# Softmax attention on one core: values projected for two groups of heads at once, laps over groups written out

## The reference

```python
H, Hk, D = (NUM_HEADS, NUM_KV_HEADS, HEAD_DIM)      # 16, 4, 128
G = H // Hk
xq = (inputs_q @ wq + bq).reshape(B, S, H, D)
xk = (inputs_q @ wk + bk).reshape(B, S, Hk, D)
xv = (inputs_q @ wv + bv).reshape(B, S, Hk, D)
...
qg = (xq * scale).reshape(B, S, Hk, G, D)
attn = jnp.einsum('bqhgd,bkhd->bhgqk', qg, xk)
attn = jax.nn.softmax(attn.astype(jnp.float32), axis=-1).astype(xq.dtype)
out = jnp.einsum('bhgqk,bkhd->bqhgd', attn.astype(xv.dtype), xv)
out = out.astype(og_dtype).reshape(B, S, H * D)
return out @ wo + bo
```

## Time and profile before

| | |
|---|---|
| time, median of 3 runs | 1144.16 us (1141.73 to 1145.95) |
| profiled execution, first to last instruction | 1142.5 us, so 1.7 us below the median |
| TensorE busy | 1058.0 us, 93% of the span |
| VectorE, ScalarE, GpSimd busy | 758.7, 599.1 and 561.4 us |
| mean granted clock of TensorE | 0.973 of full speed |

### The profile page before, as it was taken

One profiled execution on the slowest core, in us unless ns is written; L12 is line 12 of the kernel. 1 busy time (PEld: TensorE's weight loads), 2 busy tenths in 40 slices (PEclk: granted clock), 3 DMA queues, 4 the chain that ended last, 5 costly groups with the idle time before them and its releaser, 6 DMA issues. The chain is left out here.

```text
span 1142.5 us, 18205 instructions
## 1 busy us (share of the span) xinstructions
PE 1058.0 (93%) x6276; PEld 891.7 (78%) x6276; DVE 758.7 (66%) x1312; ACT 599.1 (52%) x1027; POOL 561.4 (49%) x408
## 2 busy tenths in 40 slices
PE   5899999999999999999998899997977988999992
PEld 4788888888888888888886776654765787999992
DVE  4877764787556775667775644466788655777777
ACT  3566653666536665446662423433532255777772
POOL 1664622756236563355540347762314776544453
PEclk9999999999999999999999999998998989999996
DMA  7700240002400762000000146641200457666666
GB/s 196 52 28 1 58 36 3 19 11 38 56 2 24 207 218 69 1 1 1 1 2 24 58 137 212 215 136 56 106 2 6 161 191 240 207 221 219 225 212 199
DMA packets 45642, 109.94 MB, mean 96 GB/s; under 512 B 8519, under 2 KB 26069, under 8 KB 43504
## 3 DMA queue, kind: packets, MB, share of 16 engines
q1 hardware_dynamic: 38640, 95.46, 30.2%
q0 software_dynamic: 6912, 13.30, 3.1%
HBM read 94.27 MB, written 41.29 MB: 119 GB/s over the span
## 5 line engine op out<-in xcount | busy, mean ns | idle before, releaser
L422 POOL TENSOR_TENSOR at_prob<-at_prob,at_inv_sum 128x1024 f32<-128x1024 f32 x128 | 243.6, 1905 | 287.9 <-DVE at_inv_sum L647 287.9
L612 ACT ACTIVATE at_pt_h<-ps 128x512 fp32r<-128x512 f32 x256 | 139.1, 596 | 148.7 <-PE ps L537 148.6
L697 DVE TENSOR_TENSOR at_pt_l<-ps,at_pt_h 128x512 fp32r<-128x512 f32 x256 | 164.6, 685 | 60.8 <-ACT at_pt_h L612 60.7
L686 DVE TENSOR_REDUCE at_neg_max<-ps 128x1 f32<-128x1024 f32 x128 | 156.1, 1220 | 42.1 <-PE ps L41 41.7
L579 ACT ACTIVATE at_prob<-ps,at_neg_max 128x1024 f32<-128x1024 f32 x128 | 143.7, 1123 | 18.1 <-DVE at_neg_max L686 18.1
L537 PE MATMUL ps<-ident,at_prob 128*128 128x128 f32 x1024 | 133.8, 274 | 3.8 <-POOL at_prob L422 3.8
L2072 POOL DMA_INDIRECT lines<-f_y,f_x_raw x96 | 95.8, 998 | 82.7 <-ACT f_y L1990 54.7
L537 PEld LDWEIGHTS ps<-ident,at_prob 128*128 128x128 f32 x1024 | 120.0, 141 | 20.9 <-POOL at_prob L422 4.7
L39 PE MATMUL ps<-at_k_h,at_q_h 128*128 128x512 f32 x256 | 108.8, 425 | 0.0
L41 PE MATMUL ps<-at_k_h,at_q_l 128*128 128x512 f32 x256 | 100.7, 393 | 0.0
L39 PE MATMUL ps<-at_pt_h,at_v_h 128*128 128x512 f32 x256 | 100.5, 393 | 0.0
(11 more groups left out here) (308 smaller groups left out, 2541.7 us busy)
## 6 DMA issues: line engine op xcount, KB each, us to landing
e_raw<-in_we SPq DMA_DIRECT2D x32, 624.0 KB, 4.2
f_cw_row<-cw SPq DMA_DIRECT2D x32, 512.0 KB, 4.7
slots<-in_empty SPq DMA_DIRECT2D x4, 3456.0 KB, 46.3
f_x_raw<-slots SPq DMA_DIRECT2D x32, 432.0 KB, 4.8
lines<-in_empty SPq DMA_DIRECT2D x3, 2048.0 KB, 33.8
f_e_raw<-in_we SPq DMA_DIRECT2D x32, 128.0 KB, 2.8
at_wq_raw<-in_wq SPq DMA_DIRECT2D x4, 512.0 KB, 3.5
at_wo_raw<-in_wo SPq DMA_DIRECT2D x4, 512.0 KB, 3.3
```

The costliest lines, as they stand in the source:

```text
L422: nc.gpsimd.tensor_tensor(prob[:, t % RING, :], prob[:, t % RING, :], inv_sum[:, t:t + 1].broadcast_to([P, T]), ALU.mult).then_inc(normed, 1)
L612: nc.scalar.activation(pt_h[:, e[1] % PT, :], turned(e[1]), ACT.Copy).then_inc(pt_high, 1)
L686: nc.vector.tensor_reduce(neg_max[:, t:t + 1], slot(n, start), AX.XY, ALU.max, negate=True).then_inc(maxed, 1)
L697: nc.vector.tensor_tensor(pt_l[:, e[1] % PT, :], turned(e[1]), pt_h[:, e[1] % PT, :].bitcast(F32), ALU.subtract).then_inc(pt_split, 1)
```

## The change

Values are projected for two groups at once. The weights of two groups lie side by side, so `v` has 256 columns a matmul and comes in two events, `("v", 0)` and `("v", 1)`, of four token tiles each, 24 matmuls each. They stand in the opening (groups 0 and 1) and in change 1 (groups 2 and 3); changes 0 and 2 have none. `v_full`, `v_h` and `v_l` hold two groups. The split `vs` is an event for each of the two: `("vs", 0)` is in the opening where it was, and in change 1 behind the second group of scores instead of near the end; `("vs", 1)` is in laps 0 and 2, behind step 32.

The loop over laps is written out on every engine, so counts are constants, and TensorE's program grows from 3268 to 4259 rows of its listing. The keys' and the values' weights are loaded and split apart, the values' for two groups. To make room, the normalised input that the first transposes read lies in the last two buffers of `prob`.

```diff
-    opening = [("k",), ("q", 0), ("v",)] + [("s", s) for s in range(LEAD)] + [("vs",)] + pair("t", 0)
-    steady = []
...
+    opening = [("k",), ("q", 0), ("v", 0), ("v", 1)] + [("s", s) for s in range(LEAD)] + [("vs", 0)] + pair("t", 0)
+
+    def steady(g):
+        events = []
+        for s in range(LEAD, STEPS, 2):
+            if (s // 2 + 2) % TT == 0 and not (g == KV - 1 and (s // 2 + 2) // TT == PER):
+                events.append(("q", (s // 2 + 2) // TT))
+            events += pair("s", s)
+            if s > LEAD:
+                events += pair("p", s - LEAD - 2)
+            events += pair("t", s - LEAD + 2)
+            if g % 2 == 0 and s == STEPS // 2:
+                events.append(("vs", 1))
+        return events
...
-    change = [("k",)] + pair("p", at) + pair("t", at + 4) + [("v",)] + pair("p", at + 2) + pair("t", at + 6)
-    for n in range(3):
-        change += pair("s", 2 * n) + pair("p", at + 4 + 2 * n) + pair("t", at + 8 + 2 * n)
-    change += pair("s", 6) + pair("p", at + 10) + pair("s", 8) + pair("p", at + 12)
-    change += [("vs",)] + pair("s", 10) + [("y", 0)] + pair("t", 0) + [("y", 1)]
+
+    def change(g):
+        projects = (g + 1) % 2 == 0
+        events = [("k",)] + pair("p", at) + pair("t", at + 4) + [("v", 0)] * projects + pair("p", at + 2) + pair("t", at + 6)
+        events += [("v", 1)] * projects
+        for n in range(3):
+            events += pair("s", 2 * n) + pair("p", at + 4 + 2 * n) + pair("t", at + 8 + 2 * n)
+            events += [("vs", 0)] * (projects and n == 1)
+        events += pair("s", 6) + pair("p", at + 10) + pair("s", 8) + pair("p", at + 12)
+        return events + pair("s", 10) + [("y", 0)] + pair("t", 0) + [("y", 1)]
...
-        def laps(eng, run):
+        def laps(run):
 
 
             run(-1, opening, 0)
-            with eng.Fori(0, KV - 1) as g:
-                run(g, steady + change, first)
-            run(KV - 1, [e for e in steady if e != ("q", PER)] + closing, first)
+            start = first
+            for g in range(KV):
+                events = steady(g) + (change(g) if g < KV - 1 else closing)
+                run(g, events, start)
+                start += len(jobs_of(events))
...
                         if e[0] == "v":
-                            for i in range(TT):
-                                toks = slice(i * P, (i + 1) * P)
+                            if e[1] == 0:
+                                pe.wait_ge(wkv_split, values_ready(own))
+                            for i in range(TT // 2):
+                                toks = slice((e[1] * TT // 2 + i) * P, (e[1] * TT // 2 + i + 1) * P)
                                 for c in range(DC):
-                                    last = product(nc, slot(n, start)[:, i // 4, (i % 4) * P:(i % 4 + 1) * P], xn_h[:, c, toks],
-                                                   xn_l[:, c, toks], wkv_h[:, 1, c, :], wkv_l[:, 1, c, :], c == 0, c == DC - 1)
+                                    last = product(nc, tokens_of(slot(n, start), i), xn_h[:, c, toks], xn_l[:, c, toks],
+                                                   wv_h[:, c, :], wv_l[:, c, :], c == 0, c == DC - 1)
...
                         if e[0] == "vs":
-                            inverts(0 if start == 0 else 3)
-                            if start:
-                                dve.wait_ge(pv_done, LIFT + STEPS * (g + 1))
-                            dve.wait_ge(v_added, own + 1)
-                            nc.vector.tensor_copy(v_h[:, :], v_full[:, :]).then_inc(v_high, 1)
...
+                            if start == 0:
+                                inverts(0)
+                            k = e[1]
+                            if k and g:
+                                dve.wait_ge(pv_done, LIFT + STEPS * g)
+                            dve.wait_ge(v_added, own // 2 * 2 + 2)
+                            nc.vector.tensor_copy(v_h[:, k, :], v_full[:, k, :]).then_inc(v_parts, 1)
```

More of the change, by code:

```diff
@@ L273, in jobs_of @@
         return [e for e in events if e[0] in "kvqy" or (e[0] == "s" and e[1] % 2 == 0)]
-    first, lap = len(jobs_of(opening)), len(jobs_of(steady + change))
-    assert lap % 2 == 0
+    first = len(jobs_of(opening))
     with ExitStack() as mem:
@@ L337, in proj_count, with v_high, v_split, keys_ready @@
             if e[0] == "k":
-                return 2 + PROJ * (g + 1) if not (isinstance(g, int) and g < 0) else 1
-            return 2 + PROJ * g + e[1] if not (isinstance(g, int) and g < 0) else 2
+                return 2 + PROJ * (g + 1) if g >= 0 else 1
+            return 2 + PROJ * g + e[1] if g >= 0 else 2
+        def v_high(k):
+            return v_parts, 2 * k + 1
+        def v_split(k):
+            return v_parts, 2 * k + 2
+        def keys_ready(g):
+            return (1, 3, 4, 6)[g]
+        def values_ready(g):
+            return (2, 5)[g // 2]
         def read_of(g, e, nxt):
@@ L345, in read_of @@
             if e[0] == "v":
-                return v_added, own + 1
+                return v_added, own + e[1] + 1
             if e[0] == "s":
@@ L466, in run @@
                 def run(g, events, start):
-                    jobs = jobs_of(events)
-                    spots = [n for n, e in enumerate(events) if e in jobs and (e[0] in "kvqy" or e[1] % 2 == 0)]
-                    before = jobs_of(steady + change)[-2:]
+                    spots = [n for n, e in enumerate(events) if jobs_of([e])]
                     n = start - 1
@@ L476, in begin @@
                             sem_, count = read_of(g, events[q], belongs_next(events, q))
-                        elif start == 0:
+                        elif g > 0:
+                            sem_, count = read_of(g - 1, ("y", k), False)
+                        else:
                             return
[L479 to L482, removed]
                         pe.wait_ge(sem_, count)
[L485 to L492, removed]
+                    if g == 0:
+                        pe.wait_ge(exped, LEAD // 2)
                     for place, e in enumerate(events):
@@ L564, in _ @@
                 norm.wait_parts(pe)
-                laps(pe, run)
+                laps(run)
                 bridge(nc, net, 4, 2)
@@ L590, in run @@
                             act.wait_ge(proj_full, count)
-                            if not (isinstance(g, int) and count == 1):
+                            if count > 1:
                                 act.wait_ge(proj_split, count - 1)
@@ L633, in _ @@
                 act.wait_ge(consts, 64)
-                laps(act, run)
+                laps(run)
             @block.vector
@@ new lines, in run @@
+                            part = slice(e[1] * BANK, (e[1] + 1) * BANK)
+                            nc.vector.tensor_tensor(v_full[:, :, part].rearrange("p g (i d) -> p i g d", d=DH),
+                                                    slot(n, start).rearrange("p n (i g d) -> p (n i) g d", g=2, d=DH),
+                                                    bv[:, own * DH:(own + 2) * DH].rearrange("p (g d) -> p g d", d=DH).unsqueeze(1)
+                                                    .broadcast_to([P, TT // 2, 2, DH]), ALU.add).then_inc(v_added, 1)
@@ L721, in _ @@
                 nc.vector.tensor_scalar(bq[:, :], bq[:, :], Q_SCALE, None, ALU.mult).then_inc(bq_scaled, 1)
-                laps(dve, run)
+                laps(run)
                 dve.wait_ge(y_added, LIFT + DC * KV)
```

128 lines of the change are left out of this document (64 added, 64 removed).

## The result

The changed kernel takes **1137.42 us** (median of 6 runs, 1135.12 to 1139.9), the kernel before 1144.61 us on the same chip (6 runs). The ratio is 0.9945 with a 95% interval of 0.9928 to 0.9963: faster by 0.55%, 7.2 us. The prediction was 1131.2 us, 12.9 us less than before. The time lies in the range, at its upper end, and about half of the forecast gain came.

A forecast was written before the change was run, and what follows sets the result against it. TensorE, busy throughout a lap's steady part, was taken to bound the attention stage. The terms -9.9 - 5.75 + 2.2 + 0.5 = -12.9 us, off the median of 1144.16, gave 1131.2 us (-1.1%), range 1126 to 1138.

The forecast's parts named there:

- at nothing: Items priced at zero, among them value weights' load and split, SyncE's loads and the normalised input kept in `prob`.
- term 2: Lap boundaries: written-out laps remove TensorE's gaps where the loop turns back, -5.75 us; bounds nothing and 5.75.
- Term 1: Value projections: two 256-wide blocks of about 5.8 us replace four of 5.39 us, net -9.9 us.
- Rival 3: Value projections: a matmul's price follows its width, so the wider blocks gain nothing; 1141.1 us, chance 0.04.
- Rival 1: Lap boundaries: the gap is a wait that stays, not the branch; 1136.9 us, chance 0.08.
- rival 4: Whole program: straight code must be fetched and stalls TensorE, about 2.0 us a stall; slower, about 1151 us, chance 0.03.
- Term 3: Changes 0 and 2: without the value block's cover TensorE waits for `pt_l`, 1.1 us each, +2.2 us.
- Rival 2: Changes 0 and 2: key chain holds up TensorE some 5 us each, removing blocks gains nothing; 1139.8 us, chance 0.05.
- Term 4: Moved splits of the values on VectorE: nothing in laps 0 and 2, some 0.5 us in change 1.
- (a): Split behind step 32 of laps 0 and 2: 1.9 us more on VectorE, costed at nothing.
- (b): Change 1's earlier split: little of its 1.9 us made up, output block waits some 0.5 us more; bounds 0 and 1.9.

The follow-up runs named there:

- a_narrow: Changed kernel with value matmuls 128 columns wide, one group after the other, 192 instead of 96; 1147.68 us, ratio 1.0034.
- b_unroll: Kernel before with its laps written out on every engine, values still 128 wide; 1141.98 us, ratio 0.9968.
- a_order: Changed kernel with the norm's two small tiles (96 bytes) allocated behind the others, not ahead of `pt_h`; 1132.24 us, ratio 0.988.
- a_pad928: Changed kernel with 928 unused bytes between the norm's small tiles and `pt_h` (distance from `v_h` 49 KiB); 1129.15 us, ratio 0.9861.
- b_pad128: Kernel before with 128 unused bytes per partition ahead of `pt_h`; 1146.39 us (one run).
- a_pad64: Changed kernel with 64 unused bytes per partition ahead of `pt_h`; 1138.56 us, ratio 0.9944.

## Why the prediction was off

**The step that failed** is none of the terms but what the sum left out: durations of matmuls that the diff doesn't touch were carried over from the old trace as they stood, and the normalised input's move into `prob` was booked "at nothing". It cost 96 bytes between `prob` and `pt_h`, and by them 768 x 6.6 ns = 5.1 us. With the distance back at a whole KiB the same kernel takes 1132.24 or 1129.15 us, where 1131.2 was forecast. That 1137.42 still lies in the range is luck: its upper end was set for a missing term 2, and term 2 came in full.

**Term 1, values (-9.9): right.** TensorE's timeline in change 1:

```profile
298.62 0.36 PE L39 MATMUL ps<-at_wv_h,xn_h 128*128 128x256 f32 x1
...
301.57 0.40 PE L39 MATMUL ps<-at_pt_h,at_v_h 128*128 128x512 f32 x1
...
303.77 0.36 PE L39 MATMUL ps<-at_wv_h,xn_h 128*128 128x256 f32 x1
...
306.72 0.39 PE L39 MATMUL ps<-at_k_h,at_q_h 128*128 128x512 f32 x1
```

Two halves of 2.95 us, 5.90 together (5.78 and 0.1 forecast). Rival 3 falls with `a_narrow`: width isn't the price here. The rule of the Trainium skill, "TensorE: Matmul & The Clock Gate", section "Back-to-back issue gap", doesn't fit this operand type: it gives 56 ns at 128 columns, where the rows have 112, and 109 ns at 256, where these blocks have 2.95 us / 24 = 123 ns with the restart. The section itself, which the prediction didn't say, gives this rule for a matmul by itself and calls it too low at few columns in a stream with weight loads, for which it has some 81 ns at 128 columns.

**Term 2, the loop (-5.75): right.** At the first boundary, timeline of TensorE:

```profile
182.92 0.37 PE L39 MATMUL ps<-at_wo_h,at_o_h 128*128 128x256 f32 x1
...
188.54 0.29 PE L41 MATMUL ps<-at_wo_h,at_o_l 128*128 128x256 f32 x1
188.67 0.39 PE L39 MATMUL ps<-xn_h,at_wq_h 128*128 128x512 f32 x1
...
191.44 0.39 PE L39 MATMUL ps<-at_k_h,at_q_h 128*128 128x512 f32 x1
```

No gap, and 8.52 us from y1 to the scores at each of the three boundaries, where it was 12.36, 10.57 and 8.59 and 8.59 was forecast; that makes 5.96 us. The granted clock doesn't fall behind the first as in the earlier trace rows: it is 1.00 over the query block. Rival 1 falls with `b_unroll`; the prediction's argument against it was not quite as strong as it says, since at the third boundary the wait for exponentials is missing too. That TensorE waited for code at the turn is argued, not shown. It would agree with the Trainium skill, "Runtime: NRT & Kernel Launch", section "Instruction fetch mechanics", by which a taken branch can force its target to be fetched before execution goes on. The same section calls the fetching of straight code mostly hidden; the stalls of 1.47 and 2.41 us above, if they are such fetches, are exceptions. So stalls like those of rival 4 came once in each straight kernel with narrow value blocks, and the changed kernel, whose blocks are wide, was free of them.

**Term 3, the lost cover (+2.2): right, a little too large.** TensorE behind the key projection of change 0:

```profile
155.90 0.40 PE L41 MATMUL ps<-at_pt_h,at_v_l 128*128 128x512 f32 x1
156.87 1.16 PE L566 MATMUL ps<-ident,at_prob 128*128 128x128 f32 x8 [0.57 <-DVE at_pt_l L729]
157.79 0.48 PE L39 MATMUL ps<-at_k_h,at_q_h 128*128 128x512 f32 x1
```

VectorE at that place makes the keys' low part and then the two `pt_l`:

```profile
154.90 1.22 DVE L685 TENSOR_TENSOR at_k_l<-at_proj,at_k_h 128x1024 fp32r<-128x1024 f32 x1 [3.06 <-ACT at_k_h L632]
156.04 1.28 DVE L729 TENSOR_TENSOR at_pt_l<-ps,at_pt_h 128x512 fp32r<-128x512 f32 x2
```

One wait of 0.57, and the second in the transposes' longer row (0.92 us from start to start instead of 0.79): six `p` and the transposes took 2.22 + 0.92 us instead of 1.41 + 0.79, so 0.94 each time where 1.1 was forecast. Rival 2 (some 5 us each) falls.

**Term 4.** (a) Behind step 32 the split costs nothing, as forecast:

```profile
90.75 0.68 DVE L709 CAST at_v_h<-at_v_full 128x1024 fp32r<-128x1024 f32 x1
91.47 1.22 DVE L711 TENSOR_TENSOR at_v_l<-at_v_full,at_v_h 128x1024 fp32r<-128x1024 f32 x1
```

VectorE did both at the short price, and TensorE has no gap there; its waits up to 600 us show none in the laps but the two of term 3, the three ahead of y0 and one of 0.3 in the closing (engine, operand and line, released by: us in total, times, the longest):

```profile
PE ps L566 <- POOL at_prob L460: 3.8, 2, 3.5
...
PE ps L39 <- ACT at_prob L608: 1.2, 3, 0.4
PE ps L566 <- DVE at_pt_l L729: 1.2, 2, 0.6
```

(b) was too dear. The wait ahead of y0 is 0.4 us in all three changes, and change 1, where 1.1 was forecast, is no worse than the two without a split. VectorE had made up the split's 1.9 us by then, so "little of the 1.9 us is made up" didn't hold. That the wait was 0.59 before has another reason: `b_unroll`, whose splits are where they were, has 0.42 in all three. In `a_order` and `a_pad928` change 1 waits 0.56 and 0.55 and the others 0.42, so there the earlier split costs 0.14 or 0.13.

In this stretch, then: forecast -13.3, measured -9.8 with `p` 5.1 us dearer. `a_pad928`, with that mended, shows -16.8 (567.45 to 550.61), 3.5 more than forecast: 2.3 in the scores and the waits ahead of y0 (179.54 to 177.73, where +0.5 was forecast), 0.8 in `p` with its waits (178.12 to 179.48, where +2.2 was forecast), 0.3 in y, and the rest in k and rounding. Most of the 2.3 is the scores' own spacing: in lap 1 from first to fourth query projection their matmuls are 243.1 ns apart on the mean in the kernel before and in the changed one, and 241.0 in `a_order` and `a_pad928`; over 732 that is 1.5 us. So the tiles' places act on scores too, which read neither `v_h` nor `pt_h`; no term has it, and why is open. That the mended kernels land so near the forecast is therefore partly luck.

The opening of the changed kernel's profile is 1.6 us longer (second query projection at 42.64 instead of 41.02), mostly in the key projection, 4.38 us instead of 2.91. That is not the change's: `b_pad128`, whose code ahead of it is that of the kernel before, took 4.18, and `a_pad64` 2.85.

## What to carry to other kernels

Durations read from an old trace hold only as long as the operands lie where they lay: when a change moves, adds or resizes a tile, look at which offsets of heavily used pairs of operands move with it, and measure the distance of untouched matmuls first when a sum doesn't come out. Small tiles belong behind the large ones, so that these keep whole KiB between them. A stretch with the same events in both kernels and nobody idle shows such a cost at 0.3 us, where the whole time needs six runs to show 5.

## What was not expected of the hardware

- The start-to-start distance of the `p` matmuls (fp32r, 512 columns) goes with the distance in a partition between the tiles they read: 228 ns at whole KiB, 231 at 128 bytes more, 233 at 32 or 160, 234 to 235 at 96. Why is open: no run separates `v_h` and `pt_h` from `v_l`, `pt_l` and `prob`, which move along. That one certain other engine has to be at work at the same time is not borne out: of the `p` matmuls of the laps with another `p` behind them (distances over 300 ns left out), those with no GpSimd instruction under way from 150 ns ahead of them to 150 ns behind are 234.6 ns apart on the mean in the changed kernel (267 of them) and 228.6 in the kernel before (284); with none of ScalarE 236.2 (187) and 228.9 (136), with none of VectorE 233.8 (20) and 230.0 (21).
- Straight code can stall TensorE by 1.47 to 2.41 us in the middle of a row of 128-column matmuls (112 ns apart), about as much as a loop's turn (1.98 and 1.75 us), and in none of the five kernels with 256-column value events (120 ns apart).
- Behind `b_unroll`'s stall of 1.47 us the granted clock was at 0.66 from 307 to 312 us, partly the lower level of 1.2 GHz, and the kernel before fell likewise behind its gap of 1.98 us; behind its gap of 1.75 us the query block shows no such stretch. Table by stretches of `b_unroll`, behind the stall:

```profile
307.00:312.00 5.00, 5.00 (x22) 4.25 (x22) 2.33 (x3) 1.20 (x2) 0.00 (x0) 0.66 0.01 3
```
